# Two of sixteen maxima a head taken as second bank plus positive part of a difference, in a fused attention and expert layer

## What is computed

```python
x = L0_attn_x
xn = _layernorm(x, axis=-1)
s = _L0_attn_ref(xn, L0_attn_w_qkv, L0_attn_w_out)
    # q, k = rope(...); scores = q @ k.T * scale; attn = softmax(scores); out = attn @ v @ w_out.T
g = _silu(_L0_ffn_ref(xn, L0_ffn_gate_w, L0_ffn_wg, L0_ffn_wu, L0_ffn_wd))
    # expert = argmax(xn @ gate_w.T); inter = relu(xn @ wg[expert])**2 * (xn @ wu[expert]); inter @ wd[expert]
x = x + s * g
return x
```

## Time and profile before

| | us |
|---|---|
| median of the 3 runs | 1458.0 (1457.97 to 1459.25) |
| the profiled execution, its own time | 1457.91 |
| its span | 1456.2 |
| tensor engine busy | 1431.8 (98%) |
| vector engine busy | 1337.8 (92%) |
| ScalarE busy | 1191.0 (82%) |
| GpSimd busy | 167.6 (12%) |
| granted tensor clock, mean | 0.997 of full speed (2.4 GHz) |

### The profile page before, as it was taken

How to read it: one execution, slowest core, us unless ns; L and a number is a source line. 1 busy time by engine, 2 the same in 40 slices (tenths; PEclk the granted TensorE clock), 3 DMA queues, 4 the chain that set the end, 5 groups by cost and what they waited for, 6 DMA issues and landing times.

```text
span 1456.2 us, 31933 instructions
## 1 busy us (share of the span) xinstructions
PE 1431.8 (98%) x11180; PEld 637.9 (44%) x11180; DVE 1337.8 (92%) x1960; ACT 1191.0 (82%) x2382; POOL 167.6 (12%) x237
## 2 busy tenths in 40 slices
PE   7999999999999999999999999999999999999988
PEld 5655444444474444444444444444444444444426
DVE  6689999999957999999999999999999999999806
ACT  3653488988878989889888988988898889889990
POOL 5333333200012221000010000000000000000110
PEclk9999999999999999999999999999999999999999
DMA  5875243427364455333333353223333532333323
GB/s 185 274 206 145 69 84 79 80 40 136 49 206 96 84 122 90 50 49 49 49 49 49 49 101 48 45 45 42 46 48 49 105 45 41 49 42 49 71 70 120
DMA packets 80347, 120.08 MB, mean 82 GB/s; under 512 B 28995, under 2 KB 66755, under 8 KB 73283
## 3 DMA queue, kind: packets, MB, share of 16 engines
q1 hardware_dynamic: 74258, 106.34, 36.9%
q0 software_dynamic: 3072, 8.39, 2.5%
q10 hardware_dynamic: 2896, 3.62, 0.7%
HBM read 77.67 MB, written 39.71 MB: 81 GB/s over the span
## 4 chain that ended last, share of the span: by engine, by line
PE 94%; ACT 2%; DVE 1%; DMA 1%; issue 1%; SPq 0%; POOL 0%; ACTq 0%; POOLq 0%
PE ps L1272 39%; PE ps L1286 37%; PE ps L1260 5%; PE ps L1188 3%; ACT arena L675 2%; PE ps L1487 2%; PE ps L1189 1%; PE ps L1221 1%; PE ps L1421 1%; PE ps L1213 1%; PE ps L1450 1%; PE ps L1376 1%; PE ps L1200 1%; PE ps L1165 0%; PE ps L1175 0%
## 5 line engine op out<-in xcount | busy, mean ns | idle before, releaser
L1260 PE MATMUL ps<-ks,qs 48*128 48x512 f32 x1984 | 687.6, 442 | 0.0
L1272 PE MATMUL ps<-qs,ks 50*128 50x512 f32 x2048 | 677.6, 434 | 1.2 <-ACT arena L656 0.5
L826 DVE TENSOR_REDUCE arena<-ps 128x1 f32<-128x512 f32 x992 | 632.0, 670 | 7.9 <-PE ps L1260 7.7
L675 ACT ACTIVATE arena<-ps 128x512 f32<-128x512 f32 x1056 | 566.5, 605 | 78.1 <-PE ps L1272 66.2
L829 DVE TENSOR_REDUCE arena<-ps 128x1 f32<-128x1024 f32 x496 | 597.8, 1205 | 1.3 <-PE ps L1260 1.3
L675 ACT ACTIVATE x_sb<-ps 128x512 f32<-128x512 f32 x992 | 535.2, 598 | 58.5 <-PE ps L1272 41.5
L1272 PEld LDWEIGHTS ps<-qs,ks 50*128 50x128 f32 x2048 | 326.7, 184 | 475.0 <-issue 172.2
L1260 PEld LDWEIGHTS ps<-ks,qs 48*128 48x128 f32 x1984 | 324.1, 184 | 10.9 <-issue 3.0
L1286 PE MATMUL ps<-arena 128*32 128x256 f32 (+1 forms) x3104 | 307.6, 468 | 5.7 <-ACT arena L675 4.1
L1286 PE MATMUL ps<-x_sb,arena 128*32 128x256 f32 (+1 forms) x2960 | 290.2, 464 | 0.0
L1286 PEld LDWEIGHTS ps<-arena 128*32 128x32 f32 x3104 | 62.3, 107 | 125.2 <-issue 125.2
(11 more groups left out here) (118 smaller groups left out, 613.9 us busy)
## 6 DMA issues: line engine op xcount, KB each, us to landing
qs<-parts_d SPq DMA_DIRECT2D x186, 128.0 KB, 4.4
ks<-parts_d SPq DMA_DIRECT2D x186, 128.0 KB, 5.1
parts_d<-arena SPq DMA_DIRECT2D x64, 256.0 KB, 2.8
xs_d<-arena SPq DMA_DIRECT2D x13, 384.0 KB, 3.6
arena<-xs_d SPq DMA_DIRECT2D x13, 384.0 KB, 3.4
ys_d<-arena SPq DMA_DIRECT2D x13, 384.0 KB, 2.8
x_sb<-in_x SPq DMA_DIRECT2D x2, 2048.0 KB, 13.1
onum_d<-arena SPq DMA_DIRECT2D x124, 32.0 KB
```

The source lines that it names most:

```text
L675: nc.scalar.activation(prob_of(pi, s, kb)[:, c * W:(c + 1) * W], ps[:, bank, :], ACT.Exp, scale=SCALE).then_inc(exp_done[bank], 1)
L826: nc.vector.tensor_reduce(most[head_slot][:, tile, u:u + 1], ps[:, AB + lo, :], AX.X, ALU.max).then_inc(a_reduced[u], 1)
L1260: ins = nc.tensor.matmul(ps[:, AB + c, :], qs[head_slot][ABASE:ABASE + KR, tile * P:(tile + 1) * P].bitcast(F32R), ks[head_slot][ABASE:ABA ...
L1272: nc.tensor.matmul(ps[:, bank, :], ks[s][at:at + KS, kb * P:(kb + 1) * P].bitcast(F32R), qs[s][at:at + KS, c * W:(c + 1) * W].bitcast(F32R ...
```

## The change

In pairs from `FB` on, steps 5 and 13 (`BY_DIFF`) treat banks 4 and 5 in another way. The tensor engine adds a second product to bank 4: minus the same rows of q, times the keys of bank 5. The bank then holds a0 - a1. ScalarE takes the positive part of it into SBUF (`over`), right after its exp of c = 0. The vector engine adds bank 5 to that, a1 + max(a0 - a1, 0) = max(a0, a1), and keeps the largest of the 512 sums, with one `tensor_tensor_reduce`. The two single maxima of that step fall away; the slot of the first in `most` holds a very low number.

GpSimd makes the negated rows of q (`minus_q`, 48 rows by two tiles a head) and writes that number (`negate`). It also takes over the high and low part of the maxima in these pairs; the vector engine keeps the maximum over groups (step 10) and the transposition, which moves from behind the last maximum of step 11 to behind its first. The 32 gathers, before in three lumps, go four at a time through the heads of pairs 3 to 6. To make room, `wo_sb` moves onto `turn` and is loaded by SP in the middle of the program, after pair 3.

```diff
+    BY_DIFF = (5, 13)
+    LOWEST = -3.0e38
+    DIFF_TILES = slice(3, 12, 8)
...
-        ARENA = 18800
+        ARENA = 18320
         arena = sb("arena", [P, ARENA])
+        minus_q = [sb(f"minus_q{i}", [P, 2, P]) for i in range(2)]
...
-        wo_sb = cut([KC, D])
+        wo_sb = turn[:, 16:32, :].rearrange("p (k t) w -> p k (t w)", k=KC)
...
+        over = turn[:, 0:16, :].rearrange("p t w -> p (t w)")
...
+        def by_difference(pi, kb):
+            return kb in BY_DIFF and not (isinstance(pi, int) and pi < FB)
...
+                    sp.wait_ge(inter_ready, NF)
+                    sp.dma_start(wo_sb, wout_in).then_inc(wo_loaded, 16)
...
-            act.dma_start(wo_sb, wout_in).then_inc(wo_loaded, 16)
...
+                        if c == 0 and by_difference(pi, kb - 1) and not (last_head(pi, 1) and (s == 1 or kb - 1 + AHEAD >= 2 * KB)):
+                            act.wait_ge(a_scored[0], pi * (2 * KB) + (s * KB + kb - 1 + AHEAD + 1 - KB))
+                            nc.scalar.activation(over, ps[:, AB, :], ACT.Relu).then_inc(a_reduced[0], 1)
...
-                    if not last_pair or (s == 0 and ahead < KB):
+                    if by_difference(pi, kb) and u < 2 and (not last_pair or (s == 0 and ahead < KB)):
+                        if u:
+                            t = g + AHEAD
+                            dve.wait_ge(a_scored[1], t + (1 - KB))
+                            dve.wait_ge(a_reduced[0], past(t + (1 - KB)))
+                            dve.sem_inc(diff_ready, 1)
+                            nc.vector.tensor_tensor_reduce(over, ps[:, AB + 1, :], over, 1.0, LOWEST, ALU.add, ALU.max,
+                                                           most[(s + 1 + ahead // KB) % 2][:, ahead % KB, 1:2]
+                                                           ).then_inc(a_reduced[1], 1)
+                    elif not last_pair or (s == 0 and ahead < KB):
                         reduce(g + AHEAD, (s + 1 + ahead // KB) % 2, ahead % KB, u)
...
+                        elif k == 0:
+                            for v in range(len(GROUPS)):
+                                dve.wait_ge(a_reduced[v], past((pi * 2 + (s + 1)) * KB))
+                            nc.vector.tensor_reduce(best_m, most[1 - s], AX.X, ALU.max).then_inc(best_ready, 1)
+                        elif k == 2:
+                            dve.wait_ge(low_ready, pi * 2 + (s + 1 - 2 * FB))
+                            dve.wait_ge(shift_loaded[s], (pi + 1) * 64)
+                            nc.vector.transpose(mrow, mpart).then_inc(mrow_ready, 1)
...
+            def negate(j, s, tiles):
+
+                pool.wait_ge(down_staged, NF // 2)
+                pool.wait_ge(a_loaded[s], j * (16 * LOADS) + 16 * LOADS)
+                TT(most[s][:, tiles, 0:1], lowest[:, 0:1].unsqueeze(1).to_broadcast([P, len(range(KB)[tiles]), 1]),
+                   nothing[:, 0:1].unsqueeze(1).to_broadcast([P, len(range(KB)[tiles]), 1]), ALU.add).then_inc(lowest_set, 1)
...
+                rows = qs[s][ABASE:ABASE + KR, :].rearrange("p (t i) -> p t i", i=P)
+                nc.gpsimd.tensor_scalar(minus_q[s][ABASE:ABASE + KR, :, :].bitcast(F32R), rows[:, DIFF_TILES, :], -1.0, None,
+                                        ALU.mult).then_inc(minus_ready, 1)
...
+            def cut_maxima(head):
+
+                n = head - 2 * FB
+                pool.wait_ge(best_ready, n)
+                pool.wait_ge(mrow_ready, head)
+                TT(mpart[:, 0:KB].bitcast(F32R), best_m, nothing, ALU.add).then_inc(high_ready, 1)
+                pool.wait_ge(high_ready, n)
+                TT(mpart[:, KB:2 * KB].bitcast(F32R), best_m, mpart[:, 0:KB], ALU.subtract).then_inc(low_ready, 1)
...
-            collect(0, SC)
-            stage(0, FB + 1, 0, FB + 1)
-            collect(SC, 2 * SC)
-            stage(0, FB + 1, 1, FB + 1)
-            collect(2 * SC, NT)
+            for j in range(FB, 2 * CP - 1):
+                for s in range(2):
+                    n = 2 * (j - FB) + s
+                    if n == 0:
+                        negate(FB, 1, slice(11, 12))
+                    negate(j + 1, s, DIFF_TILES)
+                    collect(NT * n // (2 * (2 * CP - 1 - FB)), NT * (n + 1) // (2 * (2 * CP - 1 - FB)))
+                    cut_maxima(2 * j + s + 1)
+                    stage(0, j + 1, s, j + 1)
...
+                less = minus is not None and c == 0
                 ins = nc.tensor.matmul(ps[:, AB + c, :], qs[head_slot][ABASE:ABASE + KR, tile * P:(tile + 1) * P].bitcast(F32R),
-                                       ks[head_slot][ABASE:ABASE + KR, c * W:(c + 1) * W].bitcast(F32R), start=True, stop=True)
+                                       ks[head_slot][ABASE:ABASE + KR, c * W:(c + 1) * W].bitcast(F32R), start=True, stop=not less)
+                if less:
+                    pe.wait_ge(minus_ready, minus)
+                    ins = nc.tensor.matmul(ps[:, AB, :], minus_q[head_slot][ABASE:ABASE + KR, tile // 8, :].bitcast(F32R),
+                                           ks[head_slot][ABASE:ABASE + KR, W:2 * W].bitcast(F32R), start=False, stop=True)
```

40 lines of the change are left out of this document (30 added, 10 removed).

## The result

The changed kernel takes 1475.19 us (median of 4 runs, 1472.45 to 1480.22), the kernel before 1458.33 in the same comparison: a ratio of 1.0119, with a 95% interval of 1.0095 to 1.0142. The prediction was a gain, 1455.0 us (1443 to 1464). The kernel became slower instead, and its time lies above that range. The profiled execution took 1480.22 us, with a span of 1478.5.

A forecast was written before the change was run, and what follows sets the result against it. The prediction took the vector engine as the bound, the tensor engine 1% behind. A full head changes by +0.02 + 0.01 - 0.15 = -0.12 us, -3.0 us in all, from 1458.0 to 1455.0 us (range 1443 to 1464).

The forecast's parts named there:

- The bound: Whole pair of heads: the vector engine sets the pace, with the tensor engine right behind it by 1%.
- item 1: Step 5, tensor engine: the added product takes 0.24 us, at worst 0.34, and delays the scores of c = 1.
- Item 2: Step 5, ScalarE: the positive part follows the exp of c = 0, takes another 0.6 us and ends at 649.92.
- Item 3: Step 5, vector engine: its operation starts 0.54 us after the score of c = 1 starts, after standing idle for 0.45 us.
- Item 4: Step 5, vector engine: the two-bank maximum follows the operation 0.72 us later, so the block changes by +0.02 us.
- The cuts: Two small vector-engine operations go to GpSimd, saving 0.15 us in each of 25 heads, 3.8 us.
- The gathers: GpSimd's queue: four a head at 4.0 us each, 16 us, fit into some 21 us, covered by 5 us.
- A: Rival, tensor engine gives way: scores arrive when wanted; 27 us gained, 1431, or weaker 12 us, 1446; chance 0.25.
- B: Rival, steps 5 and 13: the new operation is dearer; 0.28 us more a block, 1468.7 us, mildly 1460.8; chance 0.22.
- C: Rival, the block waits for ScalarE's positive part: exps 0.2 us later would give 1464.8 us; chance 0.13.
- the 23 us: In 49 blocks, one two-input operation of 0.72 us replaces two maxima of 1.19, saving 0.47 us each on paper.

The follow-up runs named there:

- product_only: The kernel before, with the score of c = 0 in steps 5 and 13 computed twice into the same bank; 1462.26 us.
- straight2: Changed kernel with the vector engine's pair loop written out, the semaphore increment before the two-input operation removed, and one gather in the third head; 1458.97 us.
- straight_inc: straight2 with the vector engine's semaphore increment ahead of the two-input operation kept; 1465.06 us.
- cuts_only: Changed kernel without differences, gathers spread as in straight2; GpSimd's cutting of the maxima and the moved weights load stay; 1454.94 us.
- c1_relu: straight2 with, in both blocks, the 512-wide values product behind the score of c = 1 and the positive part ahead of the exp of c = 0; 1478.48 us.
- split_a: c1_relu with the wide values product in halves, the first behind the score of c = 1, the second behind c = 3; 1485.86 us.
- split_b: split_a with the second half of the values product behind the score of c = 0 of the next step; 1499.4 us.
- no_product: Changed kernel with another gather table (still four in the third head) and the added product left out, so the output is wrong; 1461.96 us.
- even_straight: straight2 with the two differences in steps 4 and 12 instead of 5 and 13; 1469.21 us.

## Why the prediction was wrong

**The bound and item 1, right.** The vector engine sets the pace, and the added product comes 0.23 us (step 5) or 0.32 us (step 13) behind the a-score, against 0.24 in the sum and 0.34 at worst. Alone it costs 0.06 us a block (product_only).

**Item 2, right.** The positive part ends before the score has landed; leaving it out changes nothing.

**Item 3, wrong: the step that failed in the block.** "From the start of a score to the start of its reader are 0.54 us" was taken from ScalarE. On the vector engine it was 0.81. ScalarE's row was not far off in itself: straight2 shows 0.56 (820.56 to 821.12) in step 13 and 0.60 in step 5. What the prediction left out is what the vector engine's own queue has between the wait and the operation: with the semaphore increment it is 0.74 (straight_inc), with the loop's form too 0.81. In time of a head these two are 0.23 and 0.13 us, 0.12 and 0.07 a block. Here the engine is idle, and these instructions lie on the path. In an ordinary step, where it is busy, the loop's form costs nothing: 2.32 us in the changed kernel, 2.33 in straight2 (817.04 to 819.37). I had noted the increment in the diff and given it no time.

**Item 4, mis-sized on the safe side.** The operation takes 0.61 to 0.62 us to the next start, not 0.72. The lower bound was 0.68, since I added the second instruction; it runs beside the next one. The prediction quoted the rule that the pipe must be empty first (the Trainium skill, VectorE: DVE Perf Modes, The DRAIN you can't avoid) without the exception in the same section, that a next operation which is not held starts earlier. The trace agrees with the exception for this pair: the operation is 0.69 us long and followed after 0.61.

Together: 0.27 us too little in item 3 and 0.10 too much in item 4 give 0.17 a block, so step 5 should come out at 2.45 + 0.17 = 2.62, as in the row shown (its median is 2.65). In step 13 the product's 0.32 adds 0.08 and some hundredths stay unexplained (2.63 against 2.34 forecast). Even without the increment and the loop's form, two differences cost 0.16 us a head (37.70 in straight2 against 37.54), where the forecast had 0.03.

**The cuts, right.** 0.15 us a head forecast, 0.16 measured (cuts_only). The saving was simply outweighed: 37.70 - 0.16 (cuts) + 0.16 (two differences, bare) + 0.23 (increments) + 0.13 (loop) = 38.06.

**The gathers, wrong: the other step that failed.** "Covered, by 5 us" used the mean of 4.0 us a gather. In the third head they took 6.6 each, and 26.3 us do not fit into 21. The kernel before shows such a stretch too. Its SP queue issues the same two chunk loads at 537.29 and 539.44, without the weights' load, and four gathers around them take 23.9 us from the first start to the next one behind them:

```profile
528.68 0.97 POOL L1094 DMA_INDIRECT gate<-ys_d,arena  x1 [2.38 <-DMA gate<-ys_d,arena]
...
552.59 0.94 POOL L1094 DMA_INDIRECT gate<-ys_d,arena  x1 [4.02 <-DMA gate<-ys_d,arena]
```

I had named this as what would make the forecast fail, yet gave it neither a price nor a chance, and I did not see that the tensor engine's pause would come with a fall of its clock, which made 9.7 us of 3.4. In the profiled execution this error is of the size of that in the blocks, 0.48 us (from -0.12 forecast to +0.36) in each of 24 heads, 11.5 us.

**Rivals.** A fell: the tensor engine has room (product_only), but none of the orders tried turned it into time (c1_relu, split_a, split_b): the scores behind came late instead. B named the right size by luck, a block 0.28 us dearer than in the sum (measured 0.29 in step 13, 0.17 in step 5). Of its two parts the later product was there in step 13 (0.08 of 0.10 us), the dear hand-over of the maximum was not. C fell in the changed kernel, and is the next to bind in no_product and even_straight.

**Where the 23 us went that the blocks save on paper.** Two independent maxima need only one score each, and the first of them runs while the second score is under way. One joint operation needs the score of c = 0, the product, the positive part and the score of c = 1, and all of this in the time for which the vector engine has other work. In step 13 of the changed kernel the chain takes 2.45 us (642.75 to 645.20) and the other work covers 1.57 of it (to 643.18 + 1.14); in even steps it is 1.50 at best against 0.9 to 1.1. Only c1_relu and the two split runs have the operation wait for almost nothing, and there the scores behind are late. Each block gives back what it saves as a wait, in odd steps for the score, in even steps for the positive part, and where both come in time, for the scores behind.

## What to carry to other kernels

When two short operations are joined into one, compare not their durations but the time from the first input's start to the joint start with the work that the engine has meanwhile: here 1.50 us of chain at best against 0.9 to 1.1 of cover in even steps. And look at what moves back when the inputs are moved forward. Count the queue's instructions between the wait and the operation, increments and register work among them: here they took the start from 0.56 or 0.60 us behind the score to 0.81. Last, check work put ahead of a critical hand-over against its slowest stretch, not against its mean.

## What the runs showed of the hardware

- The read-out of an operation's accumulator (0.08 us) starts with the next operation and takes no time of its own (645.81 twice above).
- A semaphore increment between a wait and the operation behind it cost 0.12 us of a head's time where the engine is idle (0.23 for two, straight_inc against straight2).
- Around a pause of 2.8 us the tensor engine's granted clock fell to half for some 17 us; five other executions had half clock for 3.4 to 10.2 us with pauses of 1.0 to 3.4 us. In straight2, without the pause, it stays at 1.00 there.
- An indirect gather of 128 rows landed 3.0 to 3.2 us after its issue began in quiet stretches (2.05 us of wait behind 0.94), and after 5.6 to 8.2 us in the stretch of the third head with the 128 KB and 1 MB loads of SP's queue.
